# Two-layer transformer kernel: maximum blocks handed out by work, first value product half a step later, down-weight split after the last chunk

## Chip, cores and metric

One core of a Trainium2 chip runs the whole program. The metric is the device time of one launch in microseconds, the median over runs (lower is better).

## What is computed

Two transformer layers on x of 2048 tokens by 256 features, 16 heads of 16. Both have the same frame; layer 0's attention is causal with a distance penalty, layer 1's is full; layer 0's feed-forward is a gated one of width 704, layer 1's a mixture of 8 experts (all computed, two picked per token) with a shared one, 1760 columns in all.

```python
x = L0_attn_x
for layer in (0, 1):
    mod = silu(c) @ wmod                      # shifts, scales, gates
    h = layernorm(x) * (1 + ca) + sa
    S = einsum(rows, cols) * SCALE            # layer 0: + decay, -inf above the diagonal
    x = x + ga * (softmax(S) @ V) @ o_w
    h = layernorm(x) * (1 + cb) + sb
    x = x + gb * ffn(h)                       # layer 1: shared + top-2 of 8 experts
```

## The kernel before, in words

All engines walk one written list of items, the plan that `stages()` returns: a prologue, attention of layer 0, feed-forward of layer 0, attention of layer 1, feed-forward of layer 1. Each engine takes from the list the items that concern it and works them strictly in that order; semaphores join the engines. So the order of the list is the order on PE, DVE, ACT, POOL and of the DMAs that SP issues.

**Attention.** The 2048 query rows are cut into 4 chunks of 512 and the 16 heads into 4 groups of 4, which gives 16 units per layer (unit n is chunk n // 4, group n % 4). A unit goes over key tiles of 128 in steps: 16 steps per unit in layer 1; in layer 0 4, 8, 12 and 16 steps for the units of chunk 0, 1, 2 and 3, of which the last four are diagonal ones with narrower scores. A step has two halves. In each, PE makes the scores of two heads (L876, masks L884 on the diagonal), ACT takes their exponentials (L1085), and PE multiplies the exponentials of the step before with the values (L901, `pv`, 256 queries each half). The first `pv` of a unit covers all 512 queries at once and overwrites the sum bank, so it waits until ACT has copied out the sums of the unit before (`oc`, L1100).

**Maxima.** The softmax needs each row's maximum before its scores are exponentiated. It is computed ahead of the unit in blocks: one block is two score products (L845, masks L851) of 128 rows by up to 512 keys into a two-bank slot and one DVE reduction over it (L1303). A layer-1 unit has 32 blocks, a causal one 8, 16, 24 or 32. When all of a unit's blocks are in, DVE forms the parts (`mp`, L1311 to L1316), PE transposes them (`mt`, L858), ACT copies them (L1092), and SP places them in the key rows by four DMAs (`place`, L589); the unit's scores wait for that. Two slots are shared in turn by blocks and by the small items of attention, so PE can be at most two blocks ahead of DVE.

**What sets the order around the change.** `attention_walk` (L86) puts unit n's blocks evenly over the steps between `placed_at(n - 1)` and `placed_at(n)`; `placed_at` is 6 steps before the unit, or the start of the unit before it. In layer 1 this gives 14, 19 and 27 blocks beside units 0 to 2 (56 of the 512 were done during the feed-forward before it, 24 right ahead of the first step), 32 beside each of units 3 to 13, that is 2 per step, 20 beside unit 14 and none beside unit 15. After a unit come `oc` in its successor's step 0 and the transpose and normalisation of the sums (`ft`, L911, L1277, L1278) in step 1. After the fourth unit of a chunk come the pieces of the chunk's tail in steps 2 to 6 of the next unit: back transpose (`bt`, L920), output product (`op`, L930, added to x in L1288), statistics (`st`, L1222 and L1228 on DVE, then L663 and L666 on POOL), normalisation (`nm`, L1244), transpose and modulation (`ln`, L788, L1061, and the low part L724 on POOL).

**Feed-forward of layer 1.** For the first two token chunks the shared columns go first (`hg` L942, `hid` L951, with DVE L1329, L1334, L1340), then the routed ones; between the first six of these stand the six pieces of the last attention chunk's tail. The router is DVE's L1348 to L1368 (`rt`), its transposed rows L994 and L1373 (`rw`). The down product (`dn`, L973) of chunk 0 comes after two more pairs of chunk 1. It needs the down weights: SP loads them (L549) once the last `pv` is through, and POOL multiplies them by the gate and splits them into a high and a low f16 half (`wd`, `split_down`), 14 column chunks of three instructions, L713, L714, L715. In the list `("wd", 1)` stands at the head of the stage, ahead of the tail's `st`.

## Time and profile before

| what | us |
|---|---|
| median of 3 runs (1725.63 to 1739.44) | 1729.66 |
| the profiled execution | 1732.33 |
| its span on the core | 1730.3 |
| PE busy | 1533.4 (89%) |
| DVE busy | 1207.2 (70%) |
| ACT busy | 1061.6 (61%) |
| POOL busy | 177.8 (10%) |

The profiled execution is 2.0 us longer than its span. Ends of matmuls are modelled, so PE's busy share is high also where PE sets nothing; which engine ends a wait is read stage by stage. In the trace attention of layer 0 lies at about 100 to 558 us, its feed-forward to about 755, attention of layer 1 from there to 1450, and its feed-forward from there to the end. A stretch from one copy of the sums (L1100) to the next is called a unit's time below.

### The profile page before, as it was taken

Reading aid. Unit: us, or ns where it says so; the run is one execution under the profiler, and the core shown is the slowest. Engines: PE = TensorE matmul, PEld = TensorE weight load, DVE = VectorE, ACT = ScalarE, POOL = GpSimd, SP = SyncE. Lnnn points to the kernel's source line nnn. Section 1 sums busy time; section 2 is a strip of 40 time slices with the busy share of each in tenths; the row PEclk is TensorE's granted clock in tenths of the full one; section 3 lists DMA queues with packets and bytes.
Section 4 is the critical chain, followed back from the end, with each engine's and each line's share of the span. In section 5 each row is a group of like instructions: output and inputs, shape, how many; then the busy total and the mean of one; then the engine's idle time right before and its main releaser. Section 6 shows DMA issues by size and latency. Waiting matters only on the chain.

```text
span 1730.3 us, 34346 instructions
## 1 busy us (share of the span) xinstructions
PE 1533.4 (89%) x13548; PEld 637.8 (37%) x13548; DVE 1207.2 (70%) x1494; ACT 1061.6 (61%) x2017; POOL 177.8 (10%) x208
## 2 busy tenths in 40 slices
PE   7978888988999979757999899989998998699998
PEld 5633333323333544411333332332333323255565
DVE  5567797887970437886589799979998943454533
ACT  1244666866888322215999798878887896333432
POOL 1250000000000312252000000000000002500000
PEclk9879899999999989966999999999999999799999
DMA  6630000000000021240000000000000001000000
GB/s 204 145 92 12 11 10 6 8 7 6 2 2 1 13 62 44 43 126 1 6 6 11 2 6 11 6 2 11 6 6 2 2 2 43 0 7 7 13 14 13
DMA packets 39550, 41.98 MB, mean 24 GB/s; under 512 B 7172, under 2 KB 37828, under 8 KB 39388
## 3 DMA queue, kind: packets, MB, share of 16 engines
q1 hardware_dynamic: 39396, 39.79, 8.9%
q8 instruction: 113, 1.85, 0.4%
q14 instruction: 41, 0.34, 0.1%
HBM read 29.02 MB, written 10.49 MB: 23 GB/s over the span
## 4 chain that ended last, share of the span: by engine, by line
PE 36%; DVE 18%; ACT 5%; issue 4%; POOL 3%; DMA 1%; SPq 0%; ACTq 0%; DVEq 0%; POOLq 0%
DVE mpart L1303 15%; PE psum L901 9%; PE psum L973 6%; PE psum L876 6%; PE psum L951 5%; PE psum L942 5%; PE psum L845 3%; ACT probs L1085 3%; PE psum L809 1%; POOL key_region L713 1%; PE psum L960 1%; POOL hT L724 1%; PE psum L930 1%; POOL v_region L715 1%; PE psum L788 1%
## 5 line engine op out<-in xcount | busy, mean ns | idle before, releaser
L1303 DVE TENSOR_REDUCE mpart<-psum 128x2 f32<-128x1024 f32 (+2 forms) x832 | 915.6, 1157 | 133.9 <-PE psum L845 105.0
L1085 ACT ACTIVATE probs<-psum 128x512 f32<-128x512 f32 (+3 forms) x1664 | 844.5, 573 | 198.8 <-PE psum L876 110.2
L901 PE MATMUL psum<-probs,v_region 128*17 128x256 f32 (+2 forms) x6144 | 499.1, 397 | 13.7 <-ACT out_sb L1100 9.8
L845 PE MATMUL psum<-key_region,row_region 50*128 50x512 f16 (+3 forms) x1664 | 326.1, 384 | 84.1 <-DVE mpart L1303 73.9
L876 PE MATMUL psum<-row_region,key_region 52*128 52x512 f16 (+3 forms) x1664 | 358.0, 382 | 24.1 <-ACT probs L1085 16.3
L876 PEld LDWEIGHTS psum<-row_region,key_region 52*128 52x128 f16 x1664 | 98.6, 93 | 385.8 <-ACT probs L1085 290.2
L901 PEld LDWEIGHTS psum<-probs,v_region 128*17 128x17 f32 x6144 | 103.0, 95 | 208.0 <-issue 103.3
L845 PEld LDWEIGHTS psum<-key_region,row_region 50*128 50x128 f16 x1664 | 94.6, 94 | 181.3 <-DVE mpart L1303 130.8
L942 PE MATMUL psum<-hT,ffn_w 128*128 128x512 f16 (+2 forms) x480 | 121.2, 390 | 7.4 <-DVE probs L1329 6.2
L951 PE MATMUL psum<-hT,ffn_w 128*128 128x512 f16 (+2 forms) x480 | 120.6, 389 | 0.0
L1329 DVE TENSOR_TENSOR probs<-psum,probs 128x512 f32<-128x512 f32 (+1 forms) x56 | 38.7, 691 | 92.8 <-PE psum L951 87.2
L1120 ACT ACTIVATE probs<-psum 128x512 f32<-128x512 f32 (+1 forms) x56 | 33.5, 598 | 110.5 <-PE psum L942 110.5
L663 POOL TENSOR_SCALAR vare<-mv 128x4 f32<-128x4 f32 x16 | 3.6, 228 | 843.0 <-DVE mv L1228 840.3
L973 PE MATMUL psum<-v_region,key_region 128*128 128x256 f16 (+1 forms) x672 | 75.7, 276 | 3.0 <-DVE key_region L1340 3.0
L1294 DVE TENSOR_TENSOR x_sb<-psum,x_sb 128x512 f32<-128x512 f32 x16 | 11.1, 692 | 90.2 <-PE psum L973 90.2
L973 PEld LDWEIGHTS psum<-v_region,key_region 128*128 128x128 f16 (+1 forms) x672 | 66.4, 99 | 12.7 <-issue 3.5
L942 PEld LDWEIGHTS psum<-hT,ffn_w 128*128 128x128 f16 (+2 forms) x480 | 45.2, 102 | 67.8 <-issue 17.2
L951 PEld LDWEIGHTS psum<-hT,ffn_w 128*128 128x128 f16 (+2 forms) x480 | 48.1, 102 | 58.8 <-issue 7.8
L1120 ACT ACTIVATE probs<-psum,gate_s 128x512 f32<-128x512 f32 (+1 forms) x24 | 16.5, 687 | 75.6 <-PE psum L942 75.6
L1132 ACT ACTIVATE key_region<-probs 128x512 f16<-128x512 f32 (+1 forms) x80 | 49.8, 622 | 15.2 <-DVE probs L1329 8.2
L1327 DVE SCALAR_TENSOR_TENSOR probs<-psum,up_s,probs 128x512 f32<-128x512 f32 (+1 forms) x24 | 17.9, 746 | 54.6 <-PE psum L951 44.1
L1092 ACT ACTIVATE mrow_t<-psum 128x512 f16<-128x512 f32 x32 | 19.1, 598 | 57.0 <-PE psum L858 56.4
(127 smaller groups left out, 1080.9 us busy)
## 6 DMA issues: line engine op xcount, KB each, us to landing
parts<-key_region SPq DMA_DIRECT2D x32, 256.0 KB, 2.5
key_region<-parts SPq DMA_DIRECT2D x48, 128.0 KB, 4.2
row_region<-parts SPq DMA_DIRECT2D x192, 32.0 KB
key_region<-in_wmod SPq DMA_DIRECT2D x2, 1536.0 KB, 11.6
x_sb<-in_x SPq DMA_DIRECT2D x4, 512.0 KB, 8.8
row_region<-mrow_t SPq DMA_DIRECT2D x128, 2.0 KB
out<-x_sb SPq DMA_DIRECT2D x16, 128.0 KB, 1.8
key_region<-in_w_gate SPq DMA_DIRECT2D x1, 1760.0 KB, 8.8
```

Of the source, the lines that this page charges most:

```text
L845: mm = pe.matmul(bank(b + par)[:, 0:w], rows[at, g, hp, r * P:(r + 1) * P], keys[at, g * HP + hp, q * CH:q * CH + w], start=True, stop=not ...
L876: mm = pe.matmul(bank((e + par) % 3)[:, off:CH], keys[at, g * HP + hp, jt * P:(jt + 1) * P], rows[at, g, hp, off:CH], start=True, stop=not ...
L901: mm = pe.matmul(psum[32 * h:32 * h + VW, SUM_BANK, lo:hi], v_sb[:, jt, g * HG + h, :], probs[:, (S0[y] + s) % 2, h, lo:hi], start=(jt == ...
L942: mm = pe.matmul(psum[0:f, b, :], up_gate[y][0][:, u, d, c * P:c * P + f], hT16[tc][:, v, d, :], start=(m + d == 0), stop=(m + d == len(PR ...
L951: mm = pe.matmul(psum[0:f, b + 1, :], up_gate[y][1][:, u, d, c * P:c * P + f], hT16[tc][:, v, d, :], start=(m + d == 0), stop=(m + d == le ...
L973: mm = pe.matmul(bank(b)[:, r * D:(r + 1) * D], hid[y][tc % 2][0:f, c, u, tok], down[y][c][0:f, v, :], start=(c + m == 0), stop=(c + m == ...
L1085: nc.scalar.activation(probs[:, (S0[y] + s) % 2, 2 * hp + par, off:CH], psum[:, e % 3, off:CH], ACT.Exp, scale=SCALES[y]).then_inc(s_p, 1)
L1092: nc.scalar.activation(mrow_t[:, :], bank(bank_of(item)), ACT.Identity).then_inc(drained(*item)[0], 1)
L1120: nc.scalar.activation(sil[k % 2][0:f, :], psum[0:f, bank_of(("hid", y, tc, c)), :], ACT.Silu, scale=gate_s[0:f, c:c + 1] if y == 0 else 1 ...
L1132: nc.scalar.activation(hid[y][tc % 2][0:f, c, 0, :], utmp[k % 2][0:f, :], ACT.Identity).then_inc(s_hi, 1)
L1303: V.tensor_reduce(mpart[:, n % NG, at:at + 2, q:q + 1], psum[:, b:b + 2, 0:w], AX.X, ALU.max).then_inc(drained(*item)[0], 1)
L1329: ins = V.tensor_tensor(t, up, sil[k % 2][0:f, :], ALU.mult)
```

## The change

Four edits, all in the code that writes the plan.

1. `placed_at` for units with few steps: not before step 1 of the unit before (was step 0).
2. The new `spread_blocks` hands out all blocks of a layer as one queue. A block and a step each have a weight (columns of the block; columns of the step's scores); each step gets the share that the nearest due time asks for, so that shares are even over the whole layer, with two limits: a unit's blocks are all given before it is placed, and none is given before step 2 of the unit three before it, when its rows are loaded. Ahead of the first step six blocks of unit 1 stand instead of eight (both layers).
3. The first `pv` of a unit (k == 1) stands after the second scores of that step instead of between the two. `ft` and the pieces of a chunk's tail come one step later.
4. `("wd", 1)` moves from the head of the last stage to behind the sixth piece (`ln`) of the last chunk's tail.

Blocks given beside each unit, layer 1, before: 14, 19, 27, then 32 eleven times, 20, 0; now: 30, 29, 30, 30, 29, 30, 30, 29, 30, 30, 29, 30, 30, 29, 19, 0. Layer 0, before: 8, 8, 16, 11, 17, 16, 22, 18, 24, 24, 28, 28, 32, 32, 20, 0; now: 12, 11, 10, 9, 22, 19, 18, 17, 26, 26, 26, 24, 32, 32, 22, 0.

```diff
 def placed_at(y, n):
-    return max(first_step(y, n) - LEAD, first_step(y, n - 1)) if n else 0
+    return max(first_step(y, n) - LEAD, first_step(y, n - 1) + 1)
+def block_work(y, block):
+    n, r, q = block[2], block[4], block[5]
+    return 100 + 2 * ((r + 1) * P if CAUSAL[y] and q == n // NG else CH)
+def step_work(y, n, k):
+    return HG * (60 + CH - (max(0, k - TPC * (n // NG)) * P if CAUSAL[y] else 0))
+def spread_blocks(y, queue):
...
+    for s in range(placed_at(y, NU - 1)):
+        rates = [(due[n] - target) * work[s] / sum(work[s:placed_at(y, n)]) for n in range(NU) if placed_at(y, n) > s]
+        target += max(0.0, *rates) if len(rates) > 1 else max(0.0, rates[0])
+        while queue:
+            n, share = queue[0][2], block_work(y, queue[0])
+            loaded = n < NG or s >= first_step(y, n - NG + 1) + 2
+            if not (loaded and done + share // 2 <= target) and s + 1 < placed_at(y, n):
+                break
+            given[s].append(queue.pop(0))
...
-    for n in range(2 if CAUSAL[y] else 1, NU):
-        lo, hi = placed_at(y, n - 1), placed_at(y, n)
-        for m, blk in enumerate(todo[n]):
-            given[lo + (hi - lo) * m // len(todo[n])].append(blk)
...
+    out = todo[0] + [("mp", y, 0)] + todo[1][:2] + [("mt", y, 0), ("place", y, 0)] + todo[1][2:6]
+    given, ready = spread_blocks(y, todo[1][6:] + [b for part in todo[2:] for b in part])
...
-            if s:
+            if s and k != 1:
                 out.append(("pv", y, s - 1, m, j, 0))
...
-                out.append(("pv", y, s - 1, m, j, 1))
+                out.append(("pv", y, s - 1, m, j, int(k != 1)))
...
-            if k == 1 and n:
+            if k == 2 and n:
                 out.append(("ft", y, n - 1))
...
     for m, (tc, c) in enumerate([(tc, c) for tc in range(2) for c in shared]):
         out += hidden_pair(1, tc, c) + [tail(1, m)]
+        if m == 5:
+            out.append(("wd", 1))
...
-            [("load", 2), ("wf", 1)] + attention_walk(1, done), [("load", 3), ("wd", 1)] + with_halves(ffn1_walk())]
+            [("load", 2), ("wf", 1)] + attention_walk(1, done), [("load", 3)] + with_halves(ffn1_walk())]
```

PE at the start of unit 6 of layer 1, before; L901 over 17x512 is the first `pv` of the unit (it waits for `oc`), L876 are scores, L845 a maximum block, L911 the sums' transpose.

```order
L876 MATMUL psum<-row_region,key_region 128x512 x2
L845 MATMUL psum<-key_region,row_region 128x512 x2
L901 MATMUL psum<-probs,v_region 17x512 x4
L876 MATMUL psum<-row_region,key_region 128x512 x2
L845 MATMUL psum<-key_region,row_region 128x512 x2
L911 MATMUL psum<-ident,out_sb 128x128 x4
L876 MATMUL psum<-row_region,key_region 128x512 x2
```

The same place now; the same operations have the lines L896, L865, L921 and L931.

```order
L896 MATMUL psum<-row_region,key_region 128x512 x2
L865 MATMUL psum<-key_region,row_region 128x512 x2
L896 MATMUL psum<-row_region,key_region 128x512 x2
L865 MATMUL psum<-key_region,row_region 128x512 x2
L921 MATMUL psum<-probs,v_region 17x512 x4
L896 MATMUL psum<-row_region,key_region 128x512 x2
L865 MATMUL psum<-key_region,row_region 128x512 x2
L921 MATMUL psum<-probs,v_region 17x256 x4
L896 MATMUL psum<-row_region,key_region 128x512 x2
L865 MATMUL psum<-key_region,row_region 128x512 x2
L921 MATMUL psum<-probs,v_region 17x256 x4
L931 MATMUL psum<-ident,out_sb 128x128 x4
```

The second scores of the step, and the block behind them, now stand ahead of the product that waits; the sums' transpose comes a step later.

POOL at the end of attention of layer 1 and in the last stage, before: L724 is the low part of chunk 2's and then of chunk 3's features, L713 to L715 the split of the down weights, L663 and L666 the last chunk's reciprocal root.

```order
L724 TENSOR_TENSOR hT<-attn_region,hT 128x512 x2
L713 TENSOR_TENSOR key_region<-v_region,gab 128x256
L714 CAST v_region<-key_region 128x256
L715 TENSOR_TENSOR v_region<-key_region,v_region 128x256
...
L713 TENSOR_TENSOR key_region<-v_region,gab 96x256
L714 CAST v_region<-key_region 96x256
L715 TENSOR_TENSOR v_region<-key_region,v_region 96x256
L663 TENSOR_SCALAR vare<-mv 128x4
L666 TENSOR_TENSOR rstd<-vare,half 128x4
L724 TENSOR_TENSOR hT<-attn_region,hT 128x512 x2
```

The same place now, with the lines L744, L733 to L735, L683 and L686.

```order
L683 TENSOR_SCALAR vare<-mv 128x4
L686 TENSOR_TENSOR rstd<-vare,half 128x4
L744 TENSOR_TENSOR hT<-attn_region,hT 128x512 x2
L733 TENSOR_TENSOR key_region<-v_region,gab 128x256
L734 CAST v_region<-key_region 128x256
L735 TENSOR_TENSOR v_region<-key_region,v_region 128x256
...
L733 TENSOR_TENSOR key_region<-v_region,gab 96x256
L734 CAST v_region<-key_region 96x256
L735 TENSOR_TENSOR v_region<-key_region,v_region 96x256
```

The 42 instructions of the split went from ahead of the last reciprocal root to the very end of POOL's queue.

## Rows read from the trace of the kernel before

**Rows 1.** The page's costliest groups of instructions: the maximum blocks' reduction

```profile
L1303 DVE TENSOR_REDUCE mpart<-psum 128x2 f32<-128x1024 f32 (+2 forms) x832 | 915.6, 1157 | 133.9 <-PE psum L845 105.0
```

**Rows 2.** Busy time of each engine in stretches: units 2, 4, 5, 15, layer 1

```profile
core 0: us, PE busy (x) PEld busy (x) DVE busy (x) ACT busy (x) POOL busy (x), PEclk, DMA share, GB/s
874.29:910.97 36.68, 36.09 (x378) 11.74 (x374) 32.23 (x33) 34.64 (x67) 0.00 (x0) 1.00 0.03 8
949.90:1001.60 51.70, 46.55 (x420) 16.82 (x416) 42.45 (x51) 38.52 (x73) 3.54 (x4) 0.93 0.02 5
1001.60:1040.54 38.94, 37.07 (x388) 11.89 (x384) 37.61 (x38) 34.96 (x68) 0.00 (x0) 1.00 0.03 7
1416.28:1450.38 34.10, 31.42 (x316) 8.82 (x316) 0.68 (x2) 31.59 (x63) 0.00 (x0) 1.00 0.01 1
```

**Rows 3.** The chain of waits through unit 5, layer 1: start, length, what

```profile
1005.87 15.94 DVE mpart L1303 x14
```

**Rows 4.** Timeline of PE, one half step of the same unit

```profile
1016.15 0.39 PE L876 MATMUL psum<-row_region,key_region 52*128 52x512 f16 x2
...
1017.25 0.43 PE L876 MATMUL psum<-row_region,key_region 52*128 52x512 f16 x2
```

**Rows 5.** Timelines of PE and ACT where unit 5 begins

```profile
1002.35 1.05 PE L901 MATMUL psum<-probs,v_region 128*17 128x512 f32 x8 [0.40 <-ACT out_sb L1100]
1003.75 2.27 ACT L1085 ACTIVATE probs<-psum 128x512 f32<-128x512 f32 x4 [0.57 <-PE psum L876]
```

**Rows 6.** Who waited for whom, 798 to 1450 us: total, times, longest

```profile
PE psum L901 <- ACT out_sb L1100: 6.4, 15, 0.7
```

**Rows 7.** Busy time of each engine in stretches: units 2, 11, 15, layer 0

```profile
126.12:145.88 19.76, 14.71 (x156) 5.95 (x157) 16.50 (x22) 7.21 (x18) 0.00 (x0) 0.80 0.05 13
364.96:398.70 33.74, 30.49 (x342) 10.48 (x340) 29.90 (x34) 24.11 (x50) 0.00 (x0) 0.95 0.02 5
524.05:558.40 34.35, 32.64 (x327) 9.74 (x326) 0.68 (x2) 29.59 (x62) 0.00 (x0) 0.91 0.00 1
```

**Rows 8.** Timeline of POOL, 1430 to 1530 us

```profile
1459.11 1.52 POOL L713 TENSOR_TENSOR key_region<-v_region,gab 128x256 f32<-128x256 f32 x1 [140.57 <-DMA v_region<-in_w_down]
...
1481.87 0.72 POOL L713 TENSOR_TENSOR key_region<-v_region,gab 128x256 f32<-128x256 f32 x1
...
1491.79 0.22 POOL L663 TENSOR_SCALAR vare<-mv 128x4 f32<-128x4 f32 x1
1492.10 1.04 POOL L666 TENSOR_TENSOR rstd<-vare,half 128x4 f32<-128x4 f32 x1
1504.40 2.27 POOL L724 TENSOR_TENSOR hT<-attn_region,hT 128x512 f16<-128x512 f32 x2 [11.27 <-ACT hT L1061]
```

**Rows 9.** Timeline of DVE, 1430 to 1530 us

```profile
1478.99 0.38 DVE L1228 BATCH_NORM_AGGREGATE mv<-stats 128x2 f32<-128x6 f32 x4
...
1493.17 1.38 DVE L1244 TENSOR_SCALAR attn_region<-x_sb,mv,rstd 128x256 f32<-128x256 f32 x4 [12.38 <-POOL rstd L666]
```

**Rows 10.** Timeline of PE in the last stage

```profile
1470.55 2.74 PE L942 MATMUL psum<-hT,ffn_w 128*128 128x512 f16 x6 [4.11 <-DVE probs L1329]
...
1478.49 0.62 PE L994 MATMUL psum<-identb,row_region 128*24 128x128 bf16 x8
1495.19 0.60 PE L994 MATMUL psum<-identb,row_region 128*24 128x128 bf16 x4 [16.08 <-DVE row_region L1373]
```

**Rows 11.** The chain of waits, where the first down product of layer 1 begins

```profile
1542.57 18.35 PE psum L973 x168
```

**Rows 12.** Timeline of DVE: one router operation in each router part

```profile
1465.12 0.64 DVE L1359 TENSOR_TENSOR row_region<-row_region 128x96 f32<-128x96 f32 x1
...
1522.03 0.19 DVE L1359 TENSOR_TENSOR row_region<-row_region 128x32 f32<-128x32 f32 x1
```

**Rows 13.** Costliest groups of DVE, 1506.67 to 1542.57 us

```profile
L1334 DVE TENSOR_TENSOR probs<-probs 128x512 f32<-128x512 f32 x12 | 8.4, 696 | 0.4
L1340 DVE TENSOR_TENSOR key_region<-probs,key_region 128x512 f16<-128x512 f32 (+1 forms) x12 | 8.2, 683 | 0.0
```

**Rows 14.** Timeline of SP and chain of waits: placing a maximum; rows' landing

```profile
1403.86 2.38 SPq L589 DMA_DIRECT2D row_region<-mrow_t  x4
...
631.13 1.97 DMA row_region<-parts
```

More of the change, by code:

```diff
@@ L81, in placed_at @@
 def placed_at(y, n):
-    return max(first_step(y, n) - LEAD, first_step(y, n - 1)) if n else 0
+    return max(first_step(y, n) - LEAD, first_step(y, n - 1) + 1)
[5 more added lines that the diff above has]
+def spread_blocks(y, queue):
+    work = [step_work(y, n, k) for n in range(NU) for k in range(steps_of(y, n))]
+    queue = list(queue)
+    given, ready = [[] for _ in work], {}
+    due = {n: sum(block_work(y, b) for b in queue if b[2] <= n) for n in range(NU)}
+    done, target = 0, 0.0
+    for s in range(placed_at(y, NU - 1)):
[7 more added lines that the diff above has]
+            given[s].append(queue.pop(0))
+            done += share
+            if not queue or queue[0][2] != n:
+                given[s].append(("mp", y, n))
+                ready[s + 1] = ready.get(s + 1, []) + [n]
+    return given, ready
@@ L86, in attention_walk @@
 def attention_walk(y, done):
-    out = []
     todo = [[b for b in pairs_of(y, n) if b not in done] for n in range(NU)]
     total = first_step(y, NU)
-    given = [[] for _ in range(total)]
-    ready = {}
-    out += todo[0] + [("mp", y, 0)] + todo[1][:2] + [("mt", y, 0), ("place", y, 0)]
-    ahead = len(todo[1]) if CAUSAL[y] else 8
-    out += todo[1][2:ahead]
-    todo[1] = todo[1][ahead:]
-    if CAUSAL[y]:
-        out.append(("mp", y, 1))
-        ready[0] = 1
-    for n in range(2 if CAUSAL[y] else 1, NU):
-        lo, hi = placed_at(y, n - 1), placed_at(y, n)
-        for m, blk in enumerate(todo[n]):
-            given[lo + (hi - lo) * m // len(todo[n])].append(blk)
-        given[hi - 1].append(("mp", y, n))
-        ready[hi] = n
+    out = todo[0] + [("mp", y, 0)] + todo[1][:2] + [("mt", y, 0), ("place", y, 0)] + todo[1][2:6]
@@ L124, in attention_walk @@
                 out.append(("rows", y, n + 3))
-            if s in ready:
-                out += [("mt", y, ready[s]), ("place", y, ready[s])]
-            if k == 1 and n:
+            for m in ready.get(s, []):
+                out += [("mt", y, m), ("place", y, m)]
+            if k == 2 and n:
                 out.append(("ft", y, n - 1))
@@ L130, in attention_walk @@
                 i = n // NG - 1
-                if k == 2:
+                if k == 3:
                     out.append(("bt", y, i))
-                if k == 3:
+                if k == 4:
                     out.append(("op", y, i))
-                if k == 4:
+                if k == 5:
                     out.append(("st", 2 * y + 1, i))
-                if k == 5:
+                if k == 6:
                     out.append(("nm", 2 * y + 1, i))
-                if k == 6:
+                if k == 7:
                     out.append(("ln", 2 * y + 1, i))
```

## The prediction

> **What bounds the kernel now.** I read the page first, then the busy time of each engine unit by unit, then the chain of waits and the timelines where units differ. The page says only that the largest single cost is DVE's reduction of the maximum blocks, 832 of them, 915.6 us [rows 1]. Whether DVE bounds anything is seen in the units of layer 1 [rows 2]. Unit 5 has 32 blocks beside it and takes 38.94 us, with DVE busy 37.61. Unit 2 has 27 and takes 36.68, though ACT and PE do the same work but for the blocks. Unit 15 has none: 34.10 us. The chain inside unit 5 shows why the first is longer: 14 reductions back to back in 15.94 us, 1.14 us each [rows 3], while PE needs 1017.25 - 1016.15 = 1.10 us for a half step with a block in it [rows 4], and a half step without one takes 34.10 / 32 = 1.07 us. The three engines are almost level. At 32 blocks DVE sets the pace: 32 x 1.14 = 36.5, and 2.4 for the rest (normalising, parts of the maximum, idle moments). The eleven units with 32 blocks are DVE-bound; units 0, 1, 2, 14 and 15 leave DVE idle. The work is the same in sum, so evening it out is a gain.
>
> In the last stage the chain is another. PE stands still for 16.08 us until the router's rows come [rows 10]; DVE, which copies them, stands behind L1244, which waited 12.38 us for POOL's root L666 [rows 9]; and POOL started that only at 1491.79, after the whole split, which runs from 1459.11 on [rows 8]. The statistics had been ready at 1478.99 + 0.38 = 1479.37.
>
> **Even shares, layer 1.** The number of blocks beside units 3 to 13 falls from 32 to 29 or 30. For 30 blocks: by DVE 30 x 1.14 + 2.4 = 36.6; by PE, from unit 2's 36.68 with three half steps changed from 1.07 to 1.10, 36.8. At each unit's start PE waits for the copied sums (0.40, and 15 times 6.4 in all [rows 5, 6]) and ACT then 0.57 for scores that stand behind that product [rows 5]. Now these scores go first, and the copy is long done when PE comes to the product; I take off 0.4, the smaller of the two. Its price would be at the other side: the product's 1.05 us now stands ahead of the next step's scores, beside two exponentials of about 0.55 that ACT still has, so at most some 0.1 of it shows. With some friction between three engines that are now equally loaded I take 36.5, which is 2.4 less than 38.94. Eight plain units: -19.5. Units 4, 8 and 12 take 51.70 [rows 2], 12.8 more for the chunk's tail; the tail's pieces only move by one step with the same waits, and I take the same 2.4 off each: -7.3. Unit 0 goes from 14 to 30 blocks, 16 x 0.03 = 0.5, more while it starts up: +1. Units 1, 2, 14 and 15 have only the start's gain, -0.4 each: -1.6. Two blocks fewer before the first score are 2.3 us of DVE, of which the placing DMAs (2.38 to issue, about 2.0 to land [rows 14]) hide more than half: -1. Sum: -28.4. Bounds: if ACT's busy 34.96 became the pace (36.0 with its gaps closed but for 1 us) eleven units would give 2.9 each, and with 0.57 for the start 3.5, -38; if friction took half, 1.2 each, -13.
>
> **Even shares, layer 0.** Here units are short and uneven. Unit 2 (16 blocks beside it) takes 19.76 with DVE busy 16.50, unit 11 (28) 33.74 with 29.90 [rows 7]. They fall to 10 and 24 blocks. Taken by columns the reduction costs 1.14 / 512 = 0.0022 us a column: unit 2 loses 2432 columns, 5.4 us of DVE, unit 11 1920, 4.3. Where a unit is DVE-bound I take what DVE loses: unit 2 -6 (the clock granted to PE was 0.80 there, in its waits), 6 -3.5, 7 -1, 10 -1.4, 11 -4.3, 3 -1. Where blocks are added and DVE was idle part of the time I take half to all of it: units 0, 1, 4, 5, 8, 9, 14 get 3 + 3 + 2 + 1.5 + 1 + 0.7 + 1.5, minus what their idle DVE hides, 2: +10.7. Units 12 and 13 keep 32 blocks: 0. Unit 15 alone shows the floor, 34.35 for 16 steps without a block [rows 7]. The start's gain on some ten units that PE or ACT paces, 0.25 each: -2.5. A placed maximum now has three steps instead of four before short units 1 and 4. Issue and landing are 2.38 + 2.0, copying 0.6, so 5 us against two or three diagonal steps of 1.8 us: +1. Sum: -17.2 + 10.7 - 2.5 + 1 = -8. Bounds -16 and +3.
>
> **The split behind the tail.** POOL is free when the statistics are ready. Root at 1479.4 + 0.3 + 1.04 = 1480.8 instead of 1493.1: everything behind it, L1244, the rows' copy, PE's L994, moves by 12.4 us (PE still idles 3.7). That is the term: -12.4. What is late next is the split itself. It starts behind the low part of the last chunk, L724, which ended at 1506.67 [rows 8], and the first down product began at 1542.57 [rows 11]: 35.9 us between, and this distance does not move. Split as a whole took 32.7 (1459.11 to 1491.79), its nine chunks beside a busy DVE 22.76, 2.53 each, its five alone 9.92, 1.98 each [rows 8]. So 28 alone, 35.4 if all are like the busy ones: it just fits. Beside that, POOL and DVE slow each other: L1359 took 0.64 beside the split and 0.19 (a third of the elements) without [rows 12]. The first router part, on PE's path by the 4.11 us wait [rows 10], loses that drag, and the second, smaller part takes it over, some 2.8 us each way, summed over such small operations. Net 0, bounds -4 (PE also keeps its clock: L942 took 2.74 after that wait, at the lower of the two levels) and +3.
>
> The Trainium skill (page SBUF — State Buffer, section "SBUF: two separate sides") says that VectorE operations with two SBUF inputs and GpSimd operations hold the shared port pair exclusively, each for its whole instruction. By the rule as it stands the split would end late, as rival 2 works it out from rows; the trace's nine chunks beside a busy DVE do stretch, but by 0.55 us each only.
>
> **Sum.** -28.4 - 8 - 12.4 = -48.8, from the profiled 1732.33: 1683.5. The median of the runs is 2.7 lower, so 1681.
>
> **Rivals.** (1) *Three level engines lose to each other.* PE is in order with two slots; a 2-block step still makes DVE the slowest for a moment, and PE waits at every 1-to-2 change. Then a unit gives 1.2 instead of 2.4 and layer 0 -4: -13 - 2 - 4 - 12.4 = -31, 1698. The 2 are the four other units and the lead-in. For it: unit 2 with 27 blocks is already 2.6 over unit 15. Against: that is the row I took. (2) *The split ends after the down product wants it.* Place: POOL's L715 of the last chunk, with PE standing at the first L973. DVE's operations on two SBUF operands in the 35.9 us are L1334 and L1340, 8.4 + 8.2 us [rows 13], with the router's some 19 by estimate. If POOL stands through all of them, the split takes 14 x 1.98 + 19 = 46.7, 10.8 too late: -48.8 + 10.8 = -38, 1692. For it: DVE is busy throughout; against: the measured stretch of 0.55 a chunk. (3) *Slower:* the rows of a unit are loaded when the unit three before it begins, and its blocks may now come two steps later. PE's queue is in order: if issue and landing take longer than these two steps (4.4 us in layer 1), PE stands at the block, and scores, products and ACT behind it. Eight DMAs at about 0.6 and 2.0 to land are 6.8 us. The price is 2.4 per unit. The kernel is slower if it comes in more than 20 of 32 units (48.8 / 2.4); in all of them it is 77 - 49 = +28, 1758. Against: the queue of blocks is seldom three units ahead; by the counts it is so in units 0 to 4 only, and there the first four units' rows are loaded before. (4) *It does not do what it says:* the waits in the trace are ended by other semaphores than read, so that L1244 waits as long for x or for the router. Then the 12.4 don't come: 1693.
>
> **Chances.** Forecast 0.58, rival 1 0.2, rival 2 0.12, rival 4 0.06, rival 3 0.04. All bounds together are -38 - 16 - 16 = -70 and -13 + 3 - 9.4 = -19, 1660 and 1710. Both ends at once are unlikely, so the range is 1662 to 1704, which holds rivals 1, 2 and 4. A per cent is 17 us, about what a measurement here tells from no change. Faster by more: 0.95; within: 0.03; slower: 0.02.
>
> **What would show it.** Plain layer-1 units at 36.3 to 36.8 us with DVE about 35 busy, and PE's wait for L1100 gone; units 0 to 2 hardly longer; units 4, 8, 12 at 49. In layer 0 unit 2 near 13.5 and unit 11 near 29.5, units 0, 1, 4, 5 longer. PE's 16.08 us wait down to about 3.7. Wrong: units that stay at 38 with DVE idle between reductions; a wait of PE at the first down product for POOL; PE waiting for DMAs of rows.

## The result, and the profile after

The changed kernel takes 1720.5 us (median of 7 runs, 1716.96 to 1723.29), the kernel before 1732.89 beside it (7 runs): a ratio of 0.9925, with a 95% interval of 0.9901 to 0.9949. That is faster, but by 12 us where 49 were forecast, and it lies above the predicted range. The interval is half a per cent wide, finer than the per cent that the prediction took a measurement to tell. One run of all, of the experiment late_only, took 7261.1 us and is left out of what is given for that kernel below. The profiled execution took 1723.29 us, its span is 1721.5.

The page after, engines and the costliest group (it answers to [rows 1]; each line number is 20 higher than before):

```profile
PE 1536.6 (89%) x13548; PEld 636.6 (37%) x13548; DVE 1215.0 (71%) x1494; ACT 1060.7 (62%) x2017; POOL 180.5 (10%) x208
...
L1323 DVE TENSOR_REDUCE mpart<-psum 128x2 f32<-128x1024 f32 (+2 forms) x832 | 916.7, 1156 | 138.2 <-PE psum L865 108.4
```

The work is the same. A unit's time, from one copy of the sums to the next, tells where the span went:

| stretch | before | after | difference | forecast |
|---|---|---|---|---|
| up to the first copy, layer 0 | 114.43 | 119.53 | +5.1 | in layer 0 |
| units 1 to 15, layer 0 | 443.97 | 449.98 | +6.0 | -8 with the line above |
| feed-forward 0 and unit 0 of layer 1 | 279.51 | 282.26 | +2.7 | 0, in layer 1 |
| units 1 to 15, layer 1 | 612.47 | 604.40 | -8.1 | -28 with the line above |
| last copy to the end | 279.92 | 265.33 | -14.6 | -12.4 |
| span | 1730.3 | 1721.5 | -8.8 | -48.8 |

Busy time by engine after, layer 1: units 2, 5, 4 and 15 (they answer to [rows 2]) and then all of units 1 to 15 (PEclk is the granted clock):

```profile
core 0: us, PE busy (x) PEld busy (x) DVE busy (x) ACT busy (x) POOL busy (x), PEclk, DMA share, GB/s
889.77:927.61 37.84, 36.86 (x384) 12.02 (x380) 35.66 (x36) 34.56 (x67) 0.00 (x0) 1.00 0.03 7
1018.62:1056.00 37.38, 36.50 (x380) 11.82 (x376) 35.38 (x36) 34.19 (x66) 0.00 (x0) 1.00 0.05 12
965.88:1018.62 52.74, 47.81 (x414) 16.44 (x410) 39.21 (x48) 38.39 (x72) 3.54 (x4) 0.87 0.01 3
1421.96:1456.17 34.21, 31.71 (x316) 8.88 (x316) 0.68 (x2) 31.53 (x62) 0.00 (x0) 1.00 0.01 1
851.77:1456.17 604.40, 573.56 (x5693) 187.44 (x5690) 493.46 (x511) 527.52 (x1000) 10.61 (x12) 0.98 0.02 5
```

DVE is at 34.0 to 35.8 in the eight plain units of 3 to 13, about as said, but they take 37.1 to 38.3. They sum to 301.95 (37.7 each) where they were 312.04; units 1 and 2, which had been light, are 1.6 and 1.2 longer; units 4, 8 and 12 give 155.28 for 155.58. The last row for the kernel before:

```profile
837.91:1450.38 612.47, 574.64 (x5726) 187.08 (x5724) 508.96 (x528) 530.22 (x1002) 10.61 (x12) 0.99 0.02 5
```

PE was idle for 612.47 - 574.64 = 37.8 us in those fifteen units, and a gain of 28 was forecast, most of what removing every wait would give. After, it is 604.40 - 573.56 = 30.8. Who PE waits for in these units, first before and then after:

```profile
PE psum L845 <- DVE mpart L1303: 20.3, 37, 1.7
PE psum L901 <- ACT out_sb L1100: 6.4, 15, 0.7
PE psum L876 <- ACT probs L1085: 4.6, 6, 2.0
```

```profile
PE psum L896 <- ACT probs L1105: 12.7, 21, 2.0
PE psum L865 <- DVE mpart L1323: 10.1, 19, 1.7
```

The waits for DVE's reductions halved (20.3 to 10.1); the wait for the copied sums went, and the scores' wait for ACT's exponentials grew by 8.1 in its place. The start of unit 15 shows that exchange; PE first, then ACT:

```profile
1423.11 0.39 PE L896 MATMUL psum<-row_region,key_region 52*128 52x512 f16 x1 [0.59 <-ACT probs L1105]
```

```profile
1424.90 2.07 ACT L1105 ACTIVATE probs<-psum 128x512 f32<-128x512 f32 x4 [0.37 <-PE psum L896]
1427.49 2.06 ACT L1105 ACTIVATE probs<-psum 128x512 f32<-128x512 f32 x4 [0.53 <-PE psum L896]
```

The same place before:

```profile
1417.03 1.05 PE L901 MATMUL psum<-probs,v_region 128*17 128x512 f32 x8 [0.68 <-ACT out_sb L1100]
```

The scores that now stand ahead of the product need a score bank. The exponential that frees one stands on ACT behind the copy of the sums, the very copy that the product had waited for. PE waits 0.59 instead of 0.68, and ACT is idle for 0.37 and 0.53 instead of once for 0.57.

Layer 0, units 2, 11 and 15 after (they answer to [rows 7]):

```profile
134.17:147.83 13.66, 10.32 (x136) 4.37 (x134) 12.41 (x18) 6.61 (x18) 0.00 (x0) 0.94 0.14 33
373.04:405.49 32.45, 29.92 (x331) 10.12 (x329) 26.91 (x30) 24.14 (x52) 0.00 (x0) 0.95 0.03 8
534.53:569.51 34.98, 33.13 (x327) 9.80 (x326) 0.68 (x2) 29.52 (x62) 0.00 (x0) 0.90 0.00 1
```

Unit 2 came as forecast (13.5), unit 11 gave 1.3 instead of 4.3, and what was added elsewhere cost more than I had put down: unit 1 +3.0, unit 5 +4.0, unit 9 +2.6. Unit 3, which has two blocks fewer, and unit 12, which has as many as before, are longer by 1.2 and 2.4.

The last stage is the part that went to plan. POOL after, then PE and DVE (they answer to [rows 8 to 10]):

```profile
1478.07 1.04 POOL L686 TENSOR_TENSOR rstd<-vare,half 128x4 f32<-128x4 f32 x1
1489.57 2.27 POOL L744 TENSOR_TENSOR hT<-attn_region,hT 128x512 f16<-128x512 f32 x2 [10.47 <-ACT hT L1081]
1491.81 1.17 POOL L733 TENSOR_TENSOR key_region<-v_region,gab 128x256 f32<-128x256 f32 x1
...
1526.08 0.99 POOL L735 TENSOR_TENSOR v_region<-key_region,v_region 96x256 f16<-96x256 f32 x1
```

```profile
1471.64 1.47 PE L962 MATMUL psum<-hT,ffn_w 128*128 128x512 f16 x6 [1.09 <-DVE probs L1349]
1481.16 0.60 PE L1014 MATMUL psum<-identb,row_region 128*24 128x128 bf16 x4 [3.62 <-DVE row_region L1393]
1513.84 2.74 PE L962 MATMUL psum<-hT,ffn_w 128*128 128x512 f16 x6 [5.96 <-DVE probs L1349]
1533.63 1.58 PE L993 MATMUL psum<-v_region,key_region 128*128 128x256 f16 x13
```

```profile
1468.40 0.26 DVE L1379 TENSOR_TENSOR row_region<-row_region 128x96 f32<-128x96 f32 x1
1479.14 1.38 DVE L1264 TENSOR_SCALAR attn_region<-x_sb,mv,rstd 128x256 f32<-128x256 f32 x4
1529.40 0.68 DVE L1360 TENSOR_TENSOR key_region<-probs,key_region 128x512 f16<-128x512 f32 x1
```

PE waits 3.62 us for the router's rows instead of 16.08 (forecast 3.7), and 1.09 instead of 4.11 in the first router part. The second part takes the drag over: a wait of 5.96 where the kernel before had 2.12.

```profile
1524.83 1.47 PE L942 MATMUL psum<-hT,ffn_w 128*128 128x512 f16 x6 [2.12 <-DVE probs L1329]
```

The split runs from 1491.81 to 1527.07, 35.3 us (forecast 35.4), and PE reaches the first down product at 1533.63, 6.6 us later.

### The profile page after: what moved, and what is told of

The parts are those of the page before. It is cut to its first block, busy times and chain, and to the rows that moved or that the text cites. A ratio compares the mean times of both kernels' runs of the same rounds, so it can differ in the third digit from the quotient of the medians.

```text
span 1721.5 us, 34346 instructions
## 1 busy us (share of the span) xinstructions
PE 1536.6 (89%) x13548; PEld 636.6 (37%) x13548; DVE 1215.0 (71%) x1494; ACT 1060.7 (62%) x2017; POOL 180.5 (10%) x208
## 4 chain that ended last, share of the span: by engine, by line
issue 40%; PE 18%; POOL 3%; DVE 2%; DMA 1%; SPq 1%; ACT 0%; POOLq 0%; ACTq 0%; DVEq 0%
PE psum L993 6%; PE psum L962 5%; PE psum L971 5%; PE psum L829 1%; POOL hT L744 1%; POOL ffn_w L721 1%; DMA key_region<-in_w_up 1%; PE psum L980 1%; PE psum L865 0%; POOL ffn_w L720 0%; PE psum L808 0%; POOL rstd L686 0%; DMA parts<-key_region 0%; SPq L603 0%; DVE mpart L1323 0%
## 5 line engine op out<-in xcount | busy, mean ns | idle before, releaser
L921 PE MATMUL psum<-probs,v_region 128*17 128x256 f32 (+2 forms) x6144 | 503.9, 401 | 3.4 <-ACT probs L1105 0.6
L865 PE MATMUL psum<-key_region,row_region 50*128 50x512 f16 (+3 forms) x1664 | 327.4, 389 | 82.7 <-DVE mpart L1323 64.7
L896 PE MATMUL psum<-row_region,key_region 52*128 52x512 f16 (+3 forms) x1664 | 365.6, 383 | 37.2 <-ACT probs L1105 25.3
L896 PEld LDWEIGHTS psum<-row_region,key_region 52*128 52x128 f16 x1664 | 100.6, 93 | 393.1 <-ACT probs L1105 311.5
L921 PEld LDWEIGHTS psum<-probs,v_region 128*17 128x17 f32 x6144 | 102.5, 96 | 197.4 <-issue 116.2
L865 PEld LDWEIGHTS psum<-key_region,row_region 50*128 50x128 f16 x1664 | 95.3, 95 | 181.5 <-DVE mpart L1323 117.9
L962 PE MATMUL psum<-hT,ffn_w 128*128 128x512 f16 (+2 forms) x480 | 121.0, 389 | 8.2 <-DVE probs L1349 7.0
L683 POOL TENSOR_SCALAR vare<-mv 128x4 f32<-128x4 f32 x16 | 3.7, 229 | 1002.0 <-DVE mv L1248 999.4
L1349 DVE TENSOR_TENSOR probs<-psum,probs 128x512 f32<-128x512 f32 (+1 forms) x56 | 38.7, 690 | 83.2 <-PE psum L971 78.4
L1314 DVE TENSOR_TENSOR x_sb<-psum,x_sb 128x512 f32<-128x512 f32 x16 | 11.1, 691 | 91.3 <-PE psum L993 91.3
L962 PEld LDWEIGHTS psum<-hT,ffn_w 128*128 128x128 f16 (+2 forms) x480 | 45.2, 102 | 68.2 <-issue 16.5
```

Source lines behind the costliest of these rows:

```text
L865: mm = pe.matmul(bank(b + par)[:, 0:w], rows[at, g, hp, r * P:(r + 1) * P], keys[at, g * HP + hp, q * CH:q * CH + w], start=True, stop=not ...
L896: mm = pe.matmul(bank((e + par) % 3)[:, off:CH], keys[at, g * HP + hp, jt * P:(jt + 1) * P], rows[at, g, hp, off:CH], start=True, stop=not ...
L921: mm = pe.matmul(psum[32 * h:32 * h + VW, SUM_BANK, lo:hi], v_sb[:, jt, g * HG + h, :], probs[:, (S0[y] + s) % 2, h, lo:hi], start=(jt == ...
L962: mm = pe.matmul(psum[0:f, b, :], up_gate[y][0][:, u, d, c * P:c * P + f], hT16[tc][:, v, d, :], start=(m + d == 0), stop=(m + d == len(PR ...
L1349: ins = V.tensor_tensor(t, up, sil[k % 2][0:f, :], ALU.mult)
```

## Experiments

All ratios are to the kernel before, run beside each. "us" is the median.

**Each edit alone, and two together.** The three parts of the change are separable: the split's place (edit 4), the shares (edits 1 and 2), the late product and late pieces (edit 3).

```diff
# wd_only: before, and
+        if m == 5:
+            out.append(("wd", 1))
-            [("load", 3), ("wd", 1)] + with_halves(ffn1_walk())
+            [("load", 3)] + with_halves(ffn1_walk())
# shares_only: before with placed_at and spread_blocks of after
# late_only: before, and (pieces bt, op, st, nm, ln likewise)
-            if s:
+            if s and k != 1:
-                out.append(("pv", y, s - 1, m, j, 1))
+                out.append(("pv", y, s - 1, m, j, int(k != 1)))
-            if k == 1 and n:
+            if k == 2 and n:
                 out.append(("ft", y, n - 1))
# product_undone: after with all lines of late_only taken back
```

> Only the down weights' split moves behind the last chunk's tail. Both theories below agree here: the last stage was 279.9 us from the last copy of the sums to the end and is 265.3 in the changed kernel, so 14.6 us less than before, ratio about 0.9915, attention stages as before (layer 0's last copy of the sums at 558, layer 1's fifteen units 612 us).

> Only the even shares and placed_at, products and pieces where they were. Theory A (the late first product costs, the shares gain): layer 1's fifteen units from 612 to about 597, layer 0 within 3 us of before, total -10 to -15 us, ratio about 0.993. Theory B (the shares themselves lose in layer 0 and gain little in layer 1, the late product is neutral): layer 0 +9 to +11, layer 1 about -8, total 0 to +3, ratio about 1.001.

> Only the first product half a step later and the pieces a step later. Theory A: PE's wait for the copied sums (6.4 us in 15 units) turns into a wait for a score bank of about 0.6 us per unit, because the exponential that frees it stands behind the copy on ACT, and ACT idles twice at a unit's start instead of once: +0.2 to +0.5 us per unit of 32, total +6 to +15 us, ratio about 1.006. Theory B: within 3 us of before, ratio 1.000.

> The changed kernel with the first product and the pieces back where they were. Theory A: 8 to 12 us less than the changed kernel, about 1710, ratio to before about 0.986. Theory B: the same as the changed kernel, about 1720, ratio 0.9925.

| kernel | us | ratio |
|---|---|---|
| wd_only | 1718.70 | 0.9932 (0.9908 to 0.9957) |
| shares_only | 1724.57 | 0.9953 (0.9932 to 0.9975) |
| late_only | 1727.47 | 0.9966 (0.9946 to 0.9986) |
| product_undone | 1711.12 | 0.9874 (0.9846 to 0.9901) |

The split's move stands alone: wd_only's last stage is 265.39 us, and shares_only's is 277.95. In all twelve profiles with the split moved this stage takes 264.4 to 267.1 us, in the four without 277.9 to 279.9. With the shares it adds up (0.9932 x 0.9953 = 0.9885 against 0.9874 measured). Each part alone is a gain, and with the third the product would be 0.9852; all three together measured 0.9925. So edit 3 takes back some 9 us (1720.5 against 1711.1) where it stands on the even shares. By itself it seems to gain: 6.1 us by the medians without the run of 7261.1 (product_alone's expectation below says 1728.7 for it, with that run). Of the profiles' difference only 2.1 us lie in units 1 to 15 of layer 1, and most of the rest in stages that the edit doesn't touch, so this gain has no place.

**Which half of edit 3, and which layer's shares.** pieces_undone is after with `ft` and the tail's pieces back at their steps, the product still late; pieces_late the reverse. The other two have edit 3 undone whole.

```diff
# layer1_shares: after without edit 3, layer 0 with the old placed_at and old shares
 def placed_at(y, n):
+    if CAUSAL[y]:
+        return max(first_step(y, n) - LEAD, first_step(y, n - 1)) if n else 0
# two_more_ahead: after without edit 3; layer 0 has eight blocks of unit 1 ahead again
+    if CAUSAL[y]:
+        out = todo[0] + [("mp", y, 0)] + todo[1][:2] + [("mt", y, 0), ("place", y, 0)] + todo[1][2:] + [("mp", y, 1)]
+        given, ready = spread_blocks(y, [b for part in todo[2:] for b in part])
```

> The changed kernel with the sums' transpose and the tail's pieces at their old steps; the first product stays half a step later. Edit 3 as a whole costs 9.4 us beside the even shares (1720.5 against 1711.1). Theory P (the product's place costs: a second stop of ACT and a bank wait of 0.59 us at each unit's start): stays at 1718 to 1722. Theory Q (the pieces' place costs, the tails of units 4, 8, 12 in both layers and the clock after them): falls to 1710 to 1713.

> The changed kernel with the first product back between the two scores; transpose and pieces stay a step later. Theory P: 1710 to 1713, and layer 0's unit 15, which took 34.98 us at a granted clock of 0.90 in the changed kernel and 32.29 at 1.00 with edit 3 undone, is at 32.3. Theory Q: 1718 to 1722, units 4, 8, 12 of layer 1 at 51 to 53 us instead of about 49.6.

> Even shares in layer 1 only, layer 0 handed out as before; split moved; product and pieces as before. Theory C (the even shares lose in layer 0, 8.7 to 10.1 us in the profiles, and gain some 13 in layer 1): about 9 us less than with edit 3 undone alone, 1702, ratio to before about 0.982. Theory D (layer 0's loss in the profiles is the spread of the granted clock between executions, which alone moved layer 0 by 4 us in the run with only the split moved): 1709 to 1711.

> Edit 3 undone, and in layer 0 again eight instead of six blocks of unit 1 ahead of the first step, the rest evenly. PE waited 11.7 us there for the DMAs that place the first maximum, until 100.6 us, before and after alike, so blocks put there are free. If that is part of layer 0's loss, the first copy of the sums comes at about 118 instead of 120.2 us and the kernel takes about 2 us less, 1709; if not, 1711.

| kernel | us | ratio |
|---|---|---|
| pieces_undone | 1709.75 | 0.9881 (0.9851 to 0.9910) |
| pieces_late | 1718.07 | 0.9925 (0.9900 to 0.9949) |
| layer1_shares | 1702.83 | 0.9843 (0.9813 to 0.9873) |
| two_more_ahead | 1707.93 | 0.9861 (0.9841 to 0.9882) |

It is the pieces: with them late the ratio is that of the whole change, with the product alone late it is that without edit 3. No run of pieces_late (1717.0 to 1720.6) is as short as the longest of pieces_undone (1716.9). And layer 0 seems to do better with its old, uneven shares: 0.9843 against 0.9874 for product_undone, whose intervals overlap. The profiles agree: up to layer 0's last copy it is 556.16 us against 567.08. The same code up to there took 558.40 in the kernel before and 562.72 in wd_only, and that of product_undone 568.52 in shares_only, so the difference lies between 4 and 12 us.

Half of it is at the very start. The first scores of product_undone (PE, then DVE) wait for the placed maximum, and begin when they did in the kernel before, where they began at 100.67 after a wait of 7.47:

```profile
100.64 0.61 PE L896 MATMUL psum<-row_region,key_region 52*128 52x512 f16 x2 [11.68 <-DMA row_region<-mrow_t]
```

```profile
102.04 2.09 DVE L1323 TENSOR_REDUCE mpart<-psum 128x2 f32<-128x768 f32 x2 [12.34 <-PE psum L871]
```

The two blocks taken from ahead of the first score had been free, done in DVE's idle time (6.61 us there before, 12.34 now). From the first scores to the first copy it is 13.7 us with the old shares and 19.6 in product_undone, where DVE does 17 reductions in that time instead of 10. With the two blocks given back, in two_more_ahead, it is 18.3: they are worth 1.3 us there. That the first copy comes at 116.57 instead of 120.22 is for the larger part something else: the first scores began at 98.31, and in the five profiles that have product_undone's code up to there they begin anywhere from 98.8 to 102.4. Units 1 to 3 are shorter too, 35.3 to 40.6 us in sum in the four kernels with even shares and eight blocks ahead, 40.6 to 43.3 in the five with six. At the last copy of layer 0 these four stand at 556.1 to 561.4. So with the eight blocks back no profile shows that the old shares are better. In the medians the two blocks are worth 3.2 us, with intervals that overlap.

**Is the late product worth something by itself; are weights by columns the fault in layer 0?** product_alone is before with only the product late. layer1_shares_product is layer1_shares with the product late, layer0_pieces_late has also layer 0's pieces late. flat_steps is two_more_ahead with one line changed:

```diff
 def step_work(y, n, k):
-    return HG * (60 + CH - (max(0, k - TPC * (n // NG)) * P if CAUSAL[y] else 0))
+    return HG * (60 + CH)
```

> Only the first product half a step later, on the kernel before. Edit 3 alone (product and pieces) gave 1728.7 against 1733.6. If the product's move is neutral here as it was beside the even shares (1709.8 with it, 1711.1 without), 1731 to 1734; if it was what gained there, 1727 to 1729. Either way PE's wait for L1100 must be gone from the trace and a wait for a score bank of some 0.6 us stand in its place.

> The best so far (even shares in layer 1 only, split moved, pieces at their old steps, 1702.8) with the first product half a step later. Product neutral: 1701 to 1704. Product a gain of 1 to 3 us: 1699 to 1701.

> Edit 3 undone, eight blocks ahead in layer 0 (1707.9), and each step of layer 0 weighted alike, so diagonal steps get as many blocks as full ones. If the loss in layer 0 comes from the share by score columns (three blocks in full steps, one or none in diagonal ones, which leaves DVE idle there and took 39.4 instead of 38.4 us in unit 13 with the same 32 blocks), units 12 to 14 go back to 50.1, 38.4 and 36.8, layer 0 falls by 4 to 6 us, and the kernel takes 1703 to 1704. If not, 1708.

> The second of these four with transpose and tail pieces a step later in layer 0 alone, where blocks are handed out as before. If late pieces cost only where the shares are even (7 us there), this is within 2 us of that kernel; if they cost everywhere, it is 2 to 4 us slower; if they gain in layer 0's old order (edit 3 alone gained 4.9), 2 to 4 us faster.

| kernel | us | ratio |
|---|---|---|
| product_alone | 1731.33 | 0.9993 (0.9970 to 1.0016) |
| layer1_shares_product | 1709.93 | 0.9882 (0.9862 to 0.9903) |
| flat_steps | 1697.96 | 0.9810 (0.9787 to 0.9832) |
| layer0_pieces_late | 1707.24 | 0.9868 (0.9847 to 0.9889) |

The late product is worth nothing, and on layer1_shares it may even cost (0.9882 against 0.9843, intervals that overlap). Late pieces in layer 0 alone are not seen (0.9868 against 0.9882). The flat weights are a gain of 10 us over two_more_ahead, run at another time (0.9810 against 0.9861), and this is the fastest kernel. Unit 13 of layer 0 has 32 blocks in the kernel before, in after and in flat_steps. In this order:

```profile
448.78:487.22 38.44, 36.53 (x435) 13.19 (x433) 35.13 (x38) 32.55 (x68) 0.00 (x0) 1.00 0.01 2
```

```profile
457.95:497.24 39.29, 37.09 (x434) 13.19 (x432) 35.20 (x39) 32.62 (x67) 0.00 (x0) 1.00 0.01 2
```

```profile
447.79:486.21 38.42, 36.52 (x435) 13.18 (x433) 35.11 (x38) 32.53 (x67) 0.00 (x0) 1.00 0.01 2
```

The same blocks by the same engines, all at the full clock: only how they lie over the unit's steps differs. In the kernel before and in flat_steps all sixteen steps of units 12 and 13 have two. By score columns three of the twelve full steps have three, and the four narrow ones 2, 2, 1 and none. That a three-block step runs at DVE's pace while the last steps leave DVE idle is the likely reason, and no run separates it.

Where the gain lies is seen in units 9 to 14 of layer 0. They sum to 217.1, 217.3 and 218.7 us in the three kernels with flat weights and to 222.5 to 227.5 in the six with shares by columns: 3.8 us at the least, and 7.6 between flat_steps and two_more_ahead. But the whole of layer 0 doesn't show it in this pair: up to its last copy it is 556.68 us in flat_steps and 556.13 in two_more_ahead, since flat_steps began its first scores 5.1 us later, at 103.42. The 8.1 us between the two spans stand in the feed-forward of layer 0 (277.20 against 283.31) and the last stage, which the edit doesn't touch. The mean granted clock over all runs of each kernel was 0.9535 and 0.9495. So some 4 to 8 us of the 10 are the edit's, as far as the profiles tell, and the rest may be the clock of other stretches.

**The two halves of edit 3 again, on the fastest kernel.** flat_product is flat_steps with the product late, flat_pieces with `ft` and the pieces late.

> The fastest kernel so far (1698.0, ratio 0.981) with the first product half a step later. If only the pieces cost: 1697 to 1700, ratio 0.980 to 0.982. If the product costs as it seemed to beside layer 1's shares alone: 1703 to 1706, ratio 0.984 to 0.986.

> The same fastest kernel with the sums' transpose and the tail's pieces a step later and the product where it was. If the pieces cost: 1703 to 1708, ratio 0.984 to 0.987, units 4, 8 and 12 of layer 1 at 51 to 52 instead of 49.9 us each. If they don't: 1697 to 1700.

flat_product: 1702.01 us, 0.9829 (0.9807 to 0.9851). flat_pieces: 1710.22 us, 0.9883 (0.9862 to 0.9903). Against 0.9810 the product costs too little to be told from nothing, and the pieces cost 12 us. In flat_pieces the units 1 to 15 of layer 1 take 607.52 us with PE busy 577.16; in flat_steps 598.60 with 567.86. PE's idle time is the same, 30.4 and 30.7. What grew is the time that the same matmuls take. Over the twelve kernels with even shares in layer 1 PE is idle for 29.7 to 32.6 us of this stretch, and its busy time is 573.6, 574.3 and 577.2 with the pieces late, and 566.4 to 572.1 in the nine with them early. Much of that is the granted clock: PE is at the lower level for 27.3 us of the stretch in flat_pieces and for 13.7 in flat_steps (there are two levels, so a mean of 0.978 over 607.5 us is 27.3 us at half). But that pair is no proof that the order does it. Five kernels have the same code for these units (shares_only, product_undone, layer1_shares, two_more_ahead, flat_steps), and they spend 17.1, 10.2, 23.9, 13.7 and 13.7 us there; with the pieces late it is 23.9, 20.5 and 27.3. The mean granted clock over all runs is lower with the pieces late in two of three pairs: 0.948 in flat_pieces against 0.954 in flat_steps, 0.943 in the changed kernel against 0.948 in pieces_undone, but 0.950 in both pieces_late and product_undone, which are 7 us apart.

How waits and clock lie together is seen in stretches of 2 us behind the tail's transpose in unit 12, after, and then product_undone:

```profile
1322.40:1324.40 2.00, 1.50 (x15) 0.40 (x13) 1.51 (x2) 1.59 (x3) 0.00 (x0) 0.85 0.00 0
1324.40:1326.40 2.00, 1.28 (x11) 0.28 (x4) 0.77 (x1) 2.00 (x4) 0.73 (x1) 0.50 0.00 0
1326.40:1328.40 2.00, 2.00 (x15) 0.52 (x14) 1.19 (x1) 1.15 (x3) 1.54 (x2) 0.50 0.00 0
1328.40:1330.40 2.00, 2.00 (x15) 0.32 (x13) 0.73 (x2) 1.67 (x3) 0.00 (x0) 0.50 0.00 0
```

```profile
1314.50:1316.50 2.00, 2.00 (x16) 0.31 (x13) 1.81 (x2) 1.24 (x3) 0.55 (x1) 0.56 0.00 0
1316.50:1318.50 2.00, 2.00 (x18) 0.58 (x16) 1.23 (x1) 1.15 (x3) 0.00 (x0) 0.59 0.00 0
```

Behind the tail's waits PE is at the lower level (1.2 GHz) in both, after from about 1324 to 1331, in product_undone from 1314.5 to 1318. The waits ahead of it are of one size in sum, but lie otherwise, since the late pieces meet other scores and blocks (the pair differs in the product's place too):

```profile
1318.05 0.39 PE L865 MATMUL psum<-key_region,row_region 50*128 50x512 f16 x2 [1.72 <-DVE mpart L1323]
1321.60 1.09 PE L808 MATMUL psum<-ident,attn_region 128*128 128x128 f32 x8 [1.47 <-DVE mpart L1323]
1323.51 0.39 PE L865 MATMUL psum<-key_region,row_region 50*128 50x512 f16 x2 [0.50 <-DVE mpart L1323]
1326.14 0.61 PE L896 MATMUL psum<-row_region,key_region 52*128 52x512 f16 x1 [0.72 <-ACT probs L1105]
```

```profile
1305.15 0.39 PE L865 MATMUL psum<-key_region,row_region 50*128 50x512 f16 x2 [0.82 <-DVE mpart L1323]
1308.71 1.09 PE L808 MATMUL psum<-ident,attn_region 128*128 128x128 f32 x8 [1.47 <-DVE mpart L1323]
1313.25 0.39 PE L896 MATMUL psum<-row_region,key_region 52*128 52x512 f16 x1 [2.03 <-ACT probs L1105]
```

Unit 12 takes 51.04 with PE busy 45.90 in the first and 49.92 with 44.59 in the second: 1.1 us, and PE's busy time accounts for it. The three tails together take 154.8 to 155.5 us in the three kernels with late pieces and 148.8 to 153.3 in the nine with early ones, the same code five times over among them (148.8, 149.7, 150.3, 151.1, 153.3).

In the two kernels with the pieces late and the product early the plain units are longer too, 303.9 us for the eight against 301.8, at the full clock. Unit 13's start shows why, first in flat_steps, then in flat_pieces:

```profile
1326.17 0.66 PE L936 MATMUL psum<-ident,out_sb 128*128 128x128 f32 x4
1326.76 0.55 PE L901 MATMUL psum<-row_region,key_region 52*128 52x512 f16 x2
```

```profile
1341.16 0.39 PE L901 MATMUL psum<-row_region,key_region 52*128 52x512 f16 x1 [0.47 <-ACT probs L1110]
```

With the sums' transpose (L936) early it fills the time until a score bank is free. Without it the scores come to the bank sooner and wait 0.47 us, and the transpose is still to be done. The unit takes 37.68 us instead of 37.00. So it is shown that late pieces cost 7 to 12 us beside even shares, and some 2 us of that have a cause; what part the clock has is open, and so is why late pieces don't cost anything in the kernel before's own order.

## Why the prediction failed where it did

**The split behind the tail, -12.4: right.** -14.6 measured, and 13.2 between the averages of the twelve profiles with it and the four without. The root began 0.4 us behind the statistics, the wait was 3.62 for 3.7, and the split took 35.3 for 35.4. That the wait came out so exactly is in part luck: the prediction kept the statistics and PE where they were, and both came earlier, the statistics 21.1 us behind the last copy instead of 28.6, PE at L1014 20.8 instead of 28.1. The trade between the router parts came too: 3.0 us less in the first wait, 3.8 more in the second. The surplus of some 2 us is PE's clock, for which I had left up to 4: L962 took 1.47 instead of 2.74 behind the shorter wait. 1.7 of it belong to no edit, for the kernel before began the stage at the lower level (2.72 for the first L942, 1.46 after), and its 279.9 us is the longest of the four. One step was wrong to the good side: I said that the distance from the end of L724 to the first down product wouldn't move. It went from 35.9 to 41.8. The first router part, no longer beside the split, runs faster on DVE (0.26 instead of 0.64 for L1379), and so the features gain more than PE's path does.

Rival 2 is false with 6.6 us to spare, but not because the rule of the Trainium skill weighed there (page SBUF — State Buffer, section "SBUF: two separate sides") fails: the prediction read the 0.55 us a chunk as a sign against it, and the trace instruction by instruction agrees with full exclusion. DVE and POOL beside the split, after:

```profile
1494.38 0.70 DVE L1354 TENSOR_TENSOR probs<-probs 128x512 f32<-128x512 f32 x1
1494.61 1.05 POOL L733 TENSOR_TENSOR key_region<-v_region,gab 128x256 f32<-128x256 f32 x1
1495.00 1.21 DVE L1360 TENSOR_TENSOR key_region<-probs,key_region 128x512 f16<-128x512 f32 x1
1495.73 0.74 POOL L734 CAST v_region<-key_region 128x256 f16<-128x256 f32 x1
```

L733 ends 0.58 us behind the end of L1354, and L1360, begun in between, 0.55 behind the end of L733. Of the twenty L1354 and L1360 beside the split eighteen began while POOL was in an instruction, and sixteen of these end 0.54 to 0.55 us behind its end. L1349, which reads one operand from PSUM, takes 0.69 either way. What was wrong in rival 2's sum is that it had POOL stand through all of DVE's time and DVE through none of POOL's. They take turns: the split pays 2.52 - 1.98 = 0.54 a chunk, 7.5 us in all, and DVE up to 0.53 an operation (1.21 for 0.68), which is what the second router part's wait shows.

**Even shares, layer 1, -28.4: right in sign, half in size.** product_undone, with the shares and without edit 3, gives 612.47 - 597.70 = 14.8; the other four profiles with its code for these units give 10.3 to 13.9. The step that failed is "For 30 blocks: by DVE ... 36.6; by PE ... 36.8" with 36.5 taken. Each figure was a floor of one engine. In unit 2 after, with 30 blocks, PE is busy for 36.86 us, DVE for 35.66 and ACT for 34.56, and PE waits for another 1.0: it takes 37.84. On average the eight plain units came to 37.7 (37.0 at best, in flat_steps). That is the size of rival 1, which gave 1.2 a unit; 1.3 was measured. That the three level engines make each other wait is what the waits in the profile look like; no run sets it apart from other causes. "Units 0 to 2 hardly longer" failed by the same size, for these were the units that got the blocks. "I take the same 2.4 off each" tail is a step of its own: with the pieces early the three tails gave 0.8 to 2.3 us each in the profiles with product_undone's code, and in the changed kernel, with the pieces late, 0.1.

**The start of a unit, -0.4 each in layer 1, -2.5 in layer 0: wrong.** "These scores go first, and the copy is long done when PE comes to the product" holds; but the scores have a wait of their own, for the bank, behind the same copy on ACT. product_alone: 0.9993. I had looked at the product's price on the side of ACT's next exponentials, and not at what the scores needed. In product_alone's units 1 to 15 of layer 1 no wait for the copy is left, and the scores' wait for ACT is 13.4 us instead of 4.6.

**The pieces "only move by one step with the same waits": wrong.** They cost 7 to 12 us beside even shares, by pieces_late, flat_pieces and the pair after against pieces_undone. The prediction's sum had nothing for them. The waits did keep their sum in the tail (4.4 us against 4.3 in the rows above); PE's busy time in units 1 to 15 of layer 1 is what grew, by 7.1 and 9.3 us in two pairs of profiles, in part by time at the lower clock. How much of that the order does, and how much the execution, is open.

**Even shares, layer 0, -8: wrong in sign.** +11.1 after, +8.7 in product_undone. Three steps failed. "Where a unit is DVE-bound I take what DVE loses" and "minus what their idle DVE hides" treated a removed block as worth more than an added one costs: 17.2 us for nineteen removed, 10.7 for 21 added. In the profile after, the six units with fewer blocks gave 9.2 (units 3 and 10 got longer), and the seven with more took 16.4. One profile is not much for single units: unit 11 gave 1.3 there and 2.8 in product_undone. "Units 12 and 13 keep 32 blocks: 0" left out where in the unit the blocks lie, which costs 2.4 and 0.9 (1.4 and nothing with the flat weights, where 1.4 is also what unit 12 differs by between wd_only and the kernel before, with the same code). And the two blocks fewer ahead of the first score, to which nothing was charged in layer 0, were free there; they cost 1.3 us up to the first copy, and 3 in the medians, which is not clear of noise.

Rival 3 did not decide: the trace after shows no wait of PE for a DMA inside the units, and product_undone's a single one, of 2.72 us. Rival 4 is false.

## What to carry to other kernels

Before a queue is evened out, take PE's idle time in that stretch from one row: the waits can give back no more than that, and where other engines are busy for over 90% of the stretch, much less. Here it was 37.8 us, 28.4 were forecast, and 14.8 came in product_undone. Of these only 6.6 were idle time; 8.2 were busy time, from fifteen blocks that had moved ahead of unit 1 and from the clock. A wait that is ended by an engine which also frees the next thing in line moves instead of going. Judge each stage's shares by themselves: work that stands ahead of a fixed latency is free, and weights that look fairer (by columns) can put more into a step than the engine can take. Where two engines exclude each other on a port, the loss is shared between them, so it isn't to be charged to one of them whole.

## What the runs showed that I had not expected

PE's busy time isn't a constant of the work. With equal numbers of matmuls and nearly equal idle time (30.4 and 30.7 us) it was 577.2 and 567.9 us in flat_pieces and flat_steps, and from 566.4 to 572.1 us in five profiles with the same code. So one profile of a stage is good to some 5 to 7 us only: up to the last copy of layer 0 the same code took 556.2, 558.4 and 562.7 us. Unit 11 of layer 0, whose code is the same in the kernel before and in wd_only, was

```profile
366.67:402.47 35.80, 32.85 (x342) 10.79 (x340) 30.00 (x34) 24.12 (x51) 0.00 (x0) 0.86 0.02 6
```

against 33.74 at a clock of 0.95 [rows 7]: 2 us from one execution's clock. The verdicts above therefore rest on medians; the profiles say where, and only where several agree.
